# A fused decoder: the second half of a pair's scores ahead of the previous pair's weighed values

## The chip, the cores and the metric

The kernel runs on one core of one Trainium2 chip. The metric is the time of one execution in microseconds (us) on the device. The engines are TensorE (PE; PEld is its weight load), VectorE (DVE), ScalarE (ACT), GpSimd (POOL) and SyncE (SP, which issues the transfers).

## The reference, cut to what matters

Six stages follow each other, each with a residual and a layer norm: windowed self-attention (16 heads of 8), cross-attention to a context, a quantized product, a recurrence of 256 steps, a linear attention and an fp8 product. The change lies in the cross-attention of 8 batches (256 queries, 512 keys, 16 heads of 64):

```python
q = (lat @ Wq).reshape(b, n, HEADS, DHEAD).transpose(0, 2, 1, 3)
k = apply_rope(k, cos[None, None], sin[None, None])
attn = jnp.einsum('bhnd,bhsd->bhns', q, k) * scale
attn = jnp.clip(attn, -11.0, 11.0)
attn = jax.nn.softmax(attn, axis=-1)
out = jnp.einsum('bhns,bhsd->bhnd', attn, v)
```

## The kernel before, in words

Each engine has its own program, written by hand, and runs it strictly in the order written; semaphores tie the engines together. No scheduler or planner moves anything. Up to about 57 us the first batch is prepared, from 57 to 806 us the cross-attention runs, and then the later stages, which the change doesn't touch.

The cross-attention is a loop over 8 batches (0 to 7) and in each over 8 pairs of heads (0 to 7, `PAIRS`). A pair has two halves of 256 keys each. For a half, TensorE computes the scores of both heads (`unit(u)`, L2133, eight matmuls) into the same two banks, ScalarE takes the exponential (`exps(u)`, L1007) and VectorE clamps it (`clamp(u)`, L1471; the clip of the scores done behind the exponential). So `unit(1)` can only start when `exps(0)` has emptied the banks. GpSimd adds the four key blocks of the clamped tile in three additions (L731, L733, L735) to `psum`; TensorE multiplies values with the clamped tile (`values_of`, L2057) and sums `psum` over partitions (`sum_of`, L2065). VectorE divides (`attended`: reciprocal L1373, product L1374). These three work on the pair before, within the program of the current one.

Beside that, every pair prepares what later pairs need: keys of two pairs later in two products, "keys a" and "keys b" (L1758 to L1760, multiplied by cosine and sine on VectorE, L1315 and L1317, and added by GpSimd in `rotate`, L641, to `kr`), the queries of the next pair (from `lat_s`, the latents of the batch split into a high and a low part) and values. The `k_cos` and `k_sin` tiles are single, so the next `k_cos` waits for `rotate` (`kr_ready`).

In batches 0 to 6 the self-attention of the next batch is worked in between, cut into 48 slots, six for each pair: `slots(lo, hi)` stands in the pair's program on every engine and runs slots 6p+lo to 6p+hi-1 of that engine. Slots that matter here: 6, 8 and 10 (scores of the self-attention; VectorE reads them in L1251 and L1253 and frees the bank), 7 (`S_CN`: the normed context is turned and its high part kept, and VectorE makes its low part, L1305), 37 (`S_X1`: VectorE normalizes and measures x1, L1190, L1176 and L1179; GpSimd makes its reciprocal deviation, L624 and L626, and adds a bias, L692), 38 (latents normed on VectorE; GpSimd multiplies or adds a row to `k1`, L678), 40 (`S_RELU`, L1264), 43 (`S_LAT`: the latents are turned, and VectorE makes their low part, L1297, `lat_split`) and 44 (`S_KV_SUM`). The queries of the next batch's pair 0 are prepared near the end of pair 7, and wait for `lat_split`. The last batch has no slots.

Of the kernel before, what the change touches and what calls it, by code (L numbers as in the profile page):

```python
# [57 lines left out]
PER_PAIR = 6  # L58
SLOTS = PER_PAIR * PAIRS
S_X, S_K, S_Q, S_CTX, S_V = range(5)  # L60
S_CN = 7
S_MASKED = (3, 4, 5, 6)
S_SCORE = (6, 8, 10, 12, 14, 16, 18, 20)
S_EXP = (range(10, 14), range(14, 19), range(19, 24), range(24, 29))
# [115 lines left out]
def decoder(nc, a, out):  # L180
    with ExitStack() as ctx:
# [412 lines left out]
        def _(pool):  # L594
# [122 lines left out]
            def batch(b, last=False):  # L717

                for p in range(PAIRS):
                    pair = n(b, PAIRS, p)  # L720

                    def slots(lo, hi):
                        for i in range(lo, hi if not last else lo):
                            self_attention(b + 1, PER_PAIR * p + i, SELF_NORMS * (b + 1))

                    slots(0, 2)
                    pool.wait_ge(clamped, 2 * pair + 1)
                    if pair >= 2:
                        pool.wait_ge(o_full, pair - 1)
                    pp = prob[:, p % 2]  # L730
                    link(g.tensor_tensor(psum[:, p % 2, :], pp[:, 0, :], pp[:, 1, :], ALU.add))  # L731
                    pool.wait_ge(clamped, 2 * pair + 2)
                    link(g.tensor_tensor(psum[:, p % 2, :], psum[:, p % 2, :], pp[:, 2, :], ALU.add))  # L733
                    slots(2, 4)
                    g.tensor_tensor(psum[:, p % 2, :], psum[:, p % 2, :], pp[:, 3, :],  # L735
                                    ALU.add).then_inc(psum_ready, 1)
                    slots(4, 5)
                    if p + 2 < PAIRS or not last:
                        rotate(pair + 2)
                    if p == 0 and b >= 1:  # L740
                        rstd_of(b - 1, 0, QT, EPS_LN, ready=y_var_ready, done=y_rstd_ready)
                    slots(5, 6)
                    if last and p < B - 1:
                        rstd_of_f(p)
# [81 lines left out]
        def _(act):  # L826
# [170 lines left out]
            def batch(b, last=False):  # L997

                for p in range(PAIRS):
                    pair = n(b, PAIRS, p)  # L1000

                    def exps(u):
                        act.wait_ge(unit_full, 2 * pair + u + 1)

                        if pair >= 2 and u == 0:
                            act.wait_ge(o_full, pair - 1)
                        s.activation(prob[:, p % 2, 2 * u:2 * u + 2, :].rearrange("p k (h q) -> p h k q", h=2),  # L1007
                                     sc[:, 0:2, :].rearrange("p h (k q) -> p h k q", k=2), ACT.Exp,
                                     scale=DH ** -0.5).then_inc(exp_done, 1)

                    def slots(lo, hi):
                        for i in range(lo, hi if not last else lo):
                            self_attention(b + 1, PER_PAIR * p + i, SELF_NORMS * (b + 1))

                    def values_job(half):
                        if (b, p, f"values {half}") in JOB:
                            values(JOB[b, p, f"values {half}"], half)

                    exps(0)
                    slots(0, 1)  # L1020
                    slots(1, 2)
                    exps(1)
                    if p == PAIRS - 1:
                        values_job(0)
                        slots(2, 4)
                        values_job(1)
                        slots(4, 6)
                    if (b, p, "queries") in JOB:
                        queries(JOB[b, p, "queries"])
                    if p < PAIRS - 1:  # L1030
                        slots(2, 4)
                        values_job(0)
                        slots(4, 5)
                        values_job(1)
                        slots(5, 6)
                    if last and p == 1:
                        keep_turned(1, tail[:, 0:3, :].rearrange("p k d -> p (k d)"), bank_a[:, 0:3 * D])
                    if last and p >= 2:
                        keep_f(p - 2)
# [87 lines left out]
        def _(dve):  # L1127
# [97 lines left out]
            def self_attention(b, slot, norms):  # L1225
# [69 lines left out]
                if slot == S_LAT:  # L1295
                    dve.wait_ge(a_free, n(b, ACT_JOBS, SETUP_A + A_LAT + 1) if b >= 1 else FIRST_LAT)
                    w.tensor_tensor(lat_s[:, b % 2, 1, :], lat_raw[:, :], lat_s[:, b % 2, 0, :].bitcast(F32),  # L1297
                                    ALU.subtract).then_inc(lat_split, 1)
                if slot == S_CN:
                    if b == 0:  # L1300
                        dve.wait_ge(cn_kept, 1)
                    else:
# [41 lines left out]
            odd_turn(3)  # L1344
            measure_kv(0, 1)
            odd_turn(5)
            self_attention(0, S_CN, 0)
            odd_turn(7)
            odd_turn(9)
            invert_sums(0)  # L1350
# [111 lines left out]
            def batch(b, last=False):  # L1462

                for p in range(PAIRS):
# [17 lines left out]
                    keys_job("a")  # L1482
                    clamp(0)
                    slots(0, 1)
                    slots(1, 2)
                    if pair >= 1:
                        attended(pair - 1)
                    clamp(1)
                    slots(2, 3)
                    keys_job("b")  # L1490
                    slots(3, 4)
# [257 lines left out]
        def _(pe):  # L1749
# [367 lines left out]
            def batch(b, last=False):  # L2117

                for p in range(PAIRS):
# [37 lines left out]
                    unit(0)  # L2157
                    prep("keys a", prep_keys, "a")
                    slots(0, 1)
                    if pair >= 1:  # L2160
                        values_of(pair - 1)
                        sum_of(pair - 1)
                    slots(1, 2)
                    unit(1)
                    if p < PAIRS - 1:
                        prep("queries", prep_queries)
                        slots(2, 3)
# [287 lines left out]
```

## Time and profile before

| | |
|---|---|
| runs | 1050.55, 1050.72, 1046.6 us (median 1050.55) |
| profiled execution | 1047.62 us, its span 1045.9 us, mean granted clock 0.944 |
| TensorE | 919.8 us busy, 88% of the span |
| VectorE | 681.3 us, 65% |
| ScalarE | 509.6 us, 49% |
| GpSimd | 510.7 us, 49% |
| TensorE from 185 to 295 us | 103.77 of 110 us busy |

Busy shares say which engine has most work, not which wait ends last at a place; for that the timelines and waits are read. A matmul's row overlaps the next one's, since matmuls are pipelined, so work on TensorE is best measured from start to start. The granted clock is 1.00 at 2.4 GHz and 0.50 at 1.2 GHz.

### The profile page before, as it was taken

What the parts mean: (1) busy time and instruction counts of PE and PEld (TensorE: products, weight loads), DVE (VectorE), ACT (ScalarE), POOL (GpSimd) and SP (SyncE); (2) the same over time, 40 slices, a digit from 0 to 9 for tenths busy, and PEclk for the clock granted to TensorE, in tenths of its full rate; (3) what the DMA queues carried; (4) which work ended last, traced back from release to release, by engine and by line L of the source; (5) the groups of instructions that cost most, each with busy time, mean ns of one, the idle gap of its engine ahead of it and who ended that gap; (6) DMA issues with size and microseconds to landing.
All of it is one profiled execution on the core that took longest, in us unless ns stands there. A gap on an engine that the chain in (4) does not pass through costs nothing.

```text
span 1045.9 us, 22097 instructions
## 1 busy us (share of the span) xinstructions
PE 919.8 (88%) x8504; PEld 652.6 (62%) x8504; DVE 681.3 (65%) x1906; ACT 509.6 (49%) x1441; POOL 510.7 (49%) x642
## 2 busy tenths in 40 slices
PE   6689989998999999899989999998988499999922
PEld 4456656666665756566666666666656379888721
DVE  6446577568757766776687577667689543444477
ACT  6655645653663556456636645564233023333324
POOL 2643475356546534654565466446657112333363
PEclk9989999999999989999999999999999589999955
DMA  7000000000000000000000000000000001222211
GB/s 194 21 6 12 1 2 6 12 1 7 11 1 1 7 11 2 1 6 11 2 6 7 6 1 1 1 1 1 21 1 1 0 7 30 32 33 30 33 13 41
DMA packets 60470, 15.09 MB, mean 14 GB/s; under 512 B 41278, under 2 KB 59726, under 8 KB 60238
## 3 DMA queue, kind: packets, MB, share of 16 engines
q1 hardware_dynamic: 60366, 13.69, 6.1%
q8 instruction: 68, 1.11, 0.4%
q14 instruction: 36, 0.29, 0.1%
HBM read 10.51 MB, written 3.17 MB: 13 GB/s over the span
## 4 chain that ended last, share of the span: by engine, by line
PE 64%; DVE 19%; ACT 7%; POOL 5%; issue 3%; DMA 1%; SPq 0%; POOLq 0%; DVEq 0%; ACTq 0%
PE score_banks L2133 10%; PE out_bank L2057 8%; PE score_banks L1758 5%; DVE o_rec L1373 5%; PE bank_a L1753 5%; PE score_banks L2071 4%; DVE prob L1471 3%; PE score_banks L1789 3%; PE score_banks L1760 3%; PE score_banks L1759 3%; PE score_banks L2261 3%; PE bank_d L1774 3%; PE out_bank L2040 2%; PE out_bank L2065 2%; PE bank_d L2274 2%
## 5 line engine op out<-in xcount | busy, mean ns | idle before, releaser
L1007 ACT ACTIVATE prob<-score_banks 128x1024 f32<-128x1024 f32 x128 | 131.0, 1024 | 165.8 <-PE score_banks L2133 165.5
L733 POOL TENSOR_TENSOR psum<-psum,prob 128x512 f32<-128x512 f32 x64 | 81.6, 1275 | 153.9 <-DVE prob L1471 153.9
L2133 PE MATMUL score_banks<-qh,kr 64*128 64x256 f32 x1024 | 150.9, 415 | 2.1 <-ACT qh L916 1.3
L731 POOL TENSOR_TENSOR psum<-prob 128x512 f32<-128x512 f32 x64 | 82.6, 1290 | 98.4 <-DVE prob L1471 98.3
L1373 DVE RECIPROCAL o_rec<-out_bank 128x256 f32<-128x256 f32 x64 | 111.9, 1748 | 26.1 <-PE out_bank L2065 26.0
L2057 PE MATMUL out_bank<-prob,v 128*64 128x256 f32 x1024 | 124.7, 386 | 1.4 <-DVE on L1374 1.4
L2133 PEld LDWEIGHTS score_banks<-qh,kr 64*128 64x128 f32 x1024 | 91.9, 193 | 40.7 <-issue 30.5
L867 ACT ACTIVATE prob<-prob,neg_max 128x128 f32<-128x128 f32 (+1 forms) x256 | 107.1, 426 | 13.5 <-DVE neg_max L1258 13.5
L1471 DVE TENSOR_SCALAR prob<-prob 128x1024 f32<-128x1024 f32 x128 | 101.4, 792 | 12.9 <-ACT prob L1007 12.9
L2057 PEld LDWEIGHTS out_bank<-prob,v 128*64 128x64 f32 x1024 | 67.9, 136 | 46.6 <-issue 17.2
L1056 ACT ACTIVATE prob<-score_banks 128x8 f32<-128x8 f32 x255 | 45.1, 177 | 96.1 <-PE score_banks L2261 96.1
L1315 DVE TENSOR_TENSOR k_cos<-score_banks,cos_t 128x512 f32<-128x512 f32 x56 | 38.2, 682 | 72.4 <-PE score_banks L1760 46.2
L641 POOL TENSOR_TENSOR kr<-k_cos,k_sin 128x512 f32<-128x512 f32 x64 | 82.8, 1294 | 4.4 <-DVE k_sin L1317 3.6
L735 POOL TENSOR_TENSOR psum<-psum,prob 128x512 f32<-128x512 f32 x64 | 81.6, 1275 | 3.9
L2261 PE MATMUL score_banks<-prob,pt 128*64 128x8 f32 x1020 | 74.3, 210 | 0.6 <-ACT prob L1053 0.3
L835 ACT ACTIVATE pt<-bank_a 128x512 f32<-128x512 f32 x84 | 50.2, 598 | 35.5 <-PE bank_a L1753 34.6
L1774 PE MATMUL bank_d<-km,q 64*128 64x128 f32 x480 | 50.6, 330 | 17.9 <-DVE row_max L1253 16.6
L2261 PEld LDWEIGHTS score_banks<-prob,pt 128*64 128x64 f32 x1020 | 53.4, 137 | 20.8 <-ACT prob L1056 14.5
L2071 PE MATMUL score_banks<-w_qkv_t,ident 128*64 128x96 f32 (+1 forms) x336 | 64.8, 277 | 0.0
L1753 PE MATMUL bank_a<-ident,prob 128*128 128x128 f32 x360 | 57.0, 281 | 4.0 <-ACT pt L835 2.3
L1789 PE MATMUL score_banks<-pt,vm 128*32 128x128 f32 x768 | 54.0, 281 | 4.5 <-ACT pt L938 3.8
L760 POOL TENSOR_TENSOR var_eps<-mv,epsilons 128x1 f32<-128x1 f32 x49 | 9.5, 194 | 96.1 <-DVE mv L1575 96.1
(414 smaller groups left out, 2129.8 us busy)
## 6 DMA issues: line engine op xcount, KB each, us to landing
cb<-in_ctx_dram SPq DMA_DIRECT2D x8, 256.0 KB, 2.8
bias_mask<-bias_scratch SPq DMA_DIRECT2D x4, 384.0 KB, 5.4
xb<-in_x_dram SPq DMA_DIRECT2D x8, 128.0 KB, 2.1
prob<-in_L_xattn_Wkv_dram SPq DMA_DIRECT2D x1, 1024.0 KB, 8.4
x_scratch<-v SPq DMA_DIRECT2D x16, 64.0 KB, 1.5
bias_mask<-x_scratch SPq DMA_DIRECT2D x16, 64.0 KB
att_scratch<-on SPq DMA_DIRECT2D x16, 64.0 KB, 1.5
prob<-att_scratch SPq DMA_DIRECT2D x16, 64.0 KB, 3.0
```

The costliest lines, as they stand in the source:

```text
L641: g.tensor_tensor(kr[:, key % 2, :], k_cos[:, :], k_sin[:, :], ALU.add).then_inc(kr_ready, 1)
L731: link(g.tensor_tensor(psum[:, p % 2, :], pp[:, 0, :], pp[:, 1, :], ALU.add))
L867: last = s.activation(pr, pr, ACT.Exp, bias=neg_max[:, qt, j, g:g + 1], accum_out=row_sum[:, qt, j, g:g + 1])
L1007: s.activation(prob[:, p % 2, 2 * u:2 * u + 2, :].rearrange("p k (h q) -> p h k q", h=2), sc[:, 0:2, :].rearrange("p h (k q) -> p h k q", ...
L1373: link(w.reciprocal(o_rec[:, :], bank[:, T:2 * T]))
L1471: w.tensor_scalar(pr, pr, float(np.exp(-CLIP)), float(np.exp(CLIP)), ALU.max, ALU.min).then_inc(clamped, 1)
L1753: return nc.tensor.transpose(out_ap, in_ap, ident[0:in_ap.shape[0], 0:in_ap.shape[0]])
L1789: last = mm(o0_bank[32 * g:32 * g + 32, qt * P:(qt + 1) * P], vm[:, kt, j, 32 * g:32 * g + 32], pt[:, t % 2, i * P:(i + 1) * P], start=(j ...
L2057: mm(o[DH * h:DH * (h + 1), 0:T], v[:, (q // 2) % 2, kb, lo:lo + DH], prob[:, q % 2, kb, T * h:T * (h + 1)], start=(kb == 0), stop=(kb == ...
L2071: mm(bank[0:HALF_ROWS, 0:columns], ident[:, 0:HALF_ROWS], w_qkv_t[:, 0:columns], start=True, stop=True, skip_group_check=True)
L2133: last = mm(sc[:, h, k * T:(k + 1) * T], kr[rows_of, p % 2, kb * P:(kb + 1) * P], qh[rows_of, p % 2, :], start=True, stop=True, skip_group ...
L2261: last = mm(cf[lo:lo + HALF_ROWS, t * B:(t + 1) * B], a_t[:, lo:lo + HALF_ROWS], hid[:, (t - 1) * B:t * B], start=False, stop=True, skip_g ...
```

## The change

In a pair's program the second half's steps move ahead of the work on the pair before: on TensorE `unit(1)` ahead of `values_of`, `sum_of` and the pair's slot 1; on ScalarE `exps(1)` ahead of slot 1; on VectorE `clamp(1)` ahead of slot 1 and of `attended`, and `attended` ahead of slot 1. GpSimd's third addition moves ahead of the pair's slots 2 and 3. The low part of the normed context (slot 7 before) is made at slot 11 on VectorE alone. No instruction is added, removed or resized. The file is one line shorter, so behind L735 the same statement is numbered one less.

```diff
--- before.py
+++ after.py
@@ -58,7 +58,7 @@
 PER_PAIR = 6
 SLOTS = PER_PAIR * PAIRS
 S_X, S_K, S_Q, S_CTX, S_V = range(5)
-S_CN = 7
+S_CN, S_CN_LOW = 7, 11
 S_MASKED = (3, 4, 5, 6)
 S_SCORE = (6, 8, 10, 12, 14, 16, 18, 20)
 S_EXP = (range(10, 14), range(14, 19), range(19, 24), range(24, 29))
@@ -731,10 +731,9 @@
                     link(g.tensor_tensor(psum[:, p % 2, :], pp[:, 0, :], pp[:, 1, :], ALU.add))
                     pool.wait_ge(clamped, 2 * pair + 2)
                     link(g.tensor_tensor(psum[:, p % 2, :], psum[:, p % 2, :], pp[:, 2, :], ALU.add))
-                    slots(2, 4)
                     g.tensor_tensor(psum[:, p % 2, :], psum[:, p % 2, :], pp[:, 3, :],
                                     ALU.add).then_inc(psum_ready, 1)
-                    slots(4, 5)
+                    slots(2, 5)
                     if p + 2 < PAIRS or not last:
                         rotate(pair + 2)
                     if p == 0 and b >= 1:
@@ -1018,8 +1017,8 @@
 
                     exps(0)
                     slots(0, 1)
+                    exps(1)
                     slots(1, 2)
-                    exps(1)
                     if p == PAIRS - 1:
                         values_job(0)
                         slots(2, 4)
@@ -1296,7 +1295,7 @@
                     dve.wait_ge(a_free, n(b, ACT_JOBS, SETUP_A + A_LAT + 1) if b >= 1 else FIRST_LAT)
                     w.tensor_tensor(lat_s[:, b % 2, 1, :], lat_raw[:, :], lat_s[:, b % 2, 0, :].bitcast(F32),
                                     ALU.subtract).then_inc(lat_split, 1)
-                if slot == S_CN:
+                if slot == S_CN_LOW:
                     if b == 0:
                         dve.wait_ge(cn_kept, 1)
                     else:
@@ -1344,7 +1343,7 @@
             odd_turn(3)
             measure_kv(0, 1)
             odd_turn(5)
-            self_attention(0, S_CN, 0)
+            self_attention(0, S_CN_LOW, 0)
             odd_turn(7)
             odd_turn(9)
             invert_sums(0)
@@ -1482,10 +1481,10 @@
                     keys_job("a")
                     clamp(0)
                     slots(0, 1)
-                    slots(1, 2)
+                    clamp(1)
                     if pair >= 1:
                         attended(pair - 1)
-                    clamp(1)
+                    slots(1, 2)
                     slots(2, 3)
                     keys_job("b")
                     slots(3, 4)
@@ -2157,11 +2156,11 @@
                     unit(0)
                     prep("keys a", prep_keys, "a")
                     slots(0, 1)
+                    unit(1)
                     if pair >= 1:
                         values_of(pair - 1)
                         sum_of(pair - 1)
                     slots(1, 2)
-                    unit(1)
                     if p < PAIRS - 1:
                         prep("queries", prep_queries)
                         slots(2, 3)
```

VectorE in pair 6 of batch 1, before; `prob` in L1471 is the clamp, `o_rec` and `on` the division, `x` the normalization of slot 37 and `lat` that of slot 38:

```order
L1471 TENSOR_SCALAR prob<-prob 128x1024 [waits exp_done]
L1190 TENSOR_SCALAR x<-y,mv,rstd 128x128 [waits rstd_ready]
L1190 TENSOR_SCALAR x<-y,mv,rstd 128x128
L1176 BN_STATS stats<-x 128x6 [waits x1_ready]
L1176 BN_STATS stats<-x 128x6
L1179 BN_AGGR mv<-stats 128x2 [waits dve_chain]
L1179 BN_AGGR mv<-stats 128x2
L1373 RECIPROCAL o_rec<-out_bank 128x256 [waits on_ready,o_full]
L1374 TENSOR_TENSOR on<-out_bank,o_rec 128x256 [waits dve_chain]
L1471 TENSOR_SCALAR prob<-prob 128x1024 [waits exp_done]
```

After:

```order
L1470 TENSOR_SCALAR prob<-prob 128x1024 [waits exp_done] x2
L1372 RECIPROCAL o_rec<-out_bank 128x256 [waits on_ready,o_full]
L1373 TENSOR_TENSOR on<-out_bank,o_rec 128x256 [waits dve_chain]
L1189 TENSOR_SCALAR x<-y,mv,rstd 128x128 [waits rstd_ready]
L1189 TENSOR_SCALAR x<-y,mv,rstd 128x128
L1175 BN_STATS stats<-x 128x6 [waits x1_ready]
L1175 BN_STATS stats<-x 128x6
L1178 BN_AGGR mv<-stats 128x2 [waits dve_chain]
L1178 BN_AGGR mv<-stats 128x2
```

The second clamp joined the first, and the normalization and measurement of slot 37 moved behind the division.

VectorE in pair 7 of the same batch, before; `lat_s` is the low part of the latents (slot 43):

```order
L1315 TENSOR_TENSOR k_cos<-score_banks,cos_t 128x512 [waits kr_ready,p_full]
L1471 TENSOR_SCALAR prob<-prob 128x1024 [waits exp_done]
L1297 TENSOR_TENSOR lat_s<-x_t,lat_s 128x256 [waits a_free]
L1373 RECIPROCAL o_rec<-out_bank 128x256 [waits on_ready,o_full]
L1374 TENSOR_TENSOR on<-out_bank,o_rec 128x256 [waits dve_chain]
L1471 TENSOR_SCALAR prob<-prob 128x1024 [waits exp_done]
```

After:

```order
L1314 TENSOR_TENSOR k_cos<-score_banks,cos_t 128x512 [waits kr_ready,p_full]
L1470 TENSOR_SCALAR prob<-prob 128x1024 [waits exp_done] x2
L1372 RECIPROCAL o_rec<-out_bank 128x256 [waits on_ready,o_full]
L1373 TENSOR_TENSOR on<-out_bank,o_rec 128x256 [waits dve_chain]
L1296 TENSOR_TENSOR lat_s<-x_t,lat_s 128x256 [waits a_free]
```

The low part of the latents moved from ahead of the division to behind the second clamp and the division.

TensorE at the start of pair 7, before; `cn_s,wk_s` is keys a, `prob,v` the weighed values and `psum,ones` their sum of pair 6, `ident,lat` slot 43, and `qh,kr` (its last two rows) the second half's scores:

```order
L1758 MATMUL score_banks<-cn_s,wk_s 128x512 [waits p_free_by_act,cn_split]
L1759 MATMUL score_banks<-cn_s,wk_s 128x512
L1760 MATMUL score_banks<-cn_s,wk_s 128x512
L2057 MATMUL out_bank<-prob,v 64x256 [waits clamped,on_ready]
L2057 MATMUL out_bank<-prob,v 64x256 x3
L2057 MATMUL out_bank<-prob,v 64x256 [waits clamped]
L2057 MATMUL out_bank<-prob,v 64x256 x3
L2065 MATMUL out_bank<-psum,ones 64x256 [waits psum_ready]
L2065 MATMUL out_bank<-psum,ones 64x256
L1753 MATMUL bank_a<-ident,lat 128x128 [waits lat_ready,a_free]
L1753 MATMUL bank_a<-ident,lat 128x128
L2133 MATMUL score_banks<-qh,kr 128x256 [waits exp_done]
```

After:

```order
L1757 MATMUL score_banks<-cn_s,wk_s 128x512 [waits p_free_by_act,cn_split]
L1758 MATMUL score_banks<-cn_s,wk_s 128x512
L1759 MATMUL score_banks<-cn_s,wk_s 128x512
L2132 MATMUL score_banks<-qh,kr 128x256 [waits exp_done]
L2132 MATMUL score_banks<-qh,kr 128x256 x3
L2056 MATMUL out_bank<-prob,v 64x256 [waits clamped,on_ready]
L2056 MATMUL out_bank<-prob,v 64x256 x3
L2056 MATMUL out_bank<-prob,v 64x256 [waits clamped]
L2056 MATMUL out_bank<-prob,v 64x256 x3
L2064 MATMUL out_bank<-psum,ones 64x256 [waits psum_ready]
```

The second half's scores moved ahead of the values and their sum, and the wait for `exp_done` with them.

## Rows read from the trace of the kernel before

**Rows 1.** Windows of two batches: busy us of each engine, then granted clock (PEclk)
```profile
243.80:338.99 95.19, 89.28 (x690) 60.67 (x691) 66.36 (x174) 53.54 (x136) 51.65 (x54) 1.00 0.02 5
338.99:436.95 97.96, 92.20 (x690) 62.57 (x690) 66.40 (x174) 53.64 (x136) 51.65 (x54) 0.96 0.02 5
```

**Rows 2.** Waits of TensorE from 75 to 860 us: total us, times, longest
```profile
PE out_bank L2065 <- POOL psum L735: 16.7, 7, 2.4
PE bank_d L1774 <- DVE row_max L1253: 14.8, 7, 2.4
```

**Rows 3.** Timeline of TensorE: start, us, what, [idle before it <- releaser]
```profile
230.66 1.13 PE L2133 MATMUL score_banks<-qh,kr 64*128 64x256 f32 x8
...
232.61 1.95 PE L2057 MATMUL out_bank<-prob,v 128*64 128x256 f32 x16
234.39 0.60 PE L2065 MATMUL out_bank<-psum,ones 128*64 128x256 f32 x4
...
248.23 0.29 PE L1758 MATMUL score_banks<-lat_s,wq_s 128*128 128x256 f32 x1
...
249.08 0.50 PE L1758 MATMUL score_banks<-cn_s,wkx_s 128*128 128x512 f32 x1 [0.33 <-ACT v L910]
...
249.98 1.13 PE L2133 MATMUL score_banks<-qh,kr 64*128 64x256 f32 x8
```

**Rows 4.** Timeline of ScalarE: two exponentials of a pair's first half
```profile
231.84 1.03 ACT L1007 ACTIVATE prob<-score_banks 128x1024 f32<-128x1024 f32 x1 [0.92 <-PE score_banks L2133]
...
264.53 1.00 ACT L1007 ACTIVATE prob<-score_banks 128x1024 f32<-128x1024 f32 x1
```

**Rows 5.** Timeline of TensorE in pair 1 of batch 2
```profile
261.85 1.14 PE L2133 MATMUL score_banks<-qh,kr 64*128 64x256 f32 x8
...
264.56 1.95 PE L2057 MATMUL out_bank<-prob,v 128*64 128x256 f32 x16
...
273.59 0.82 PE L1774 MATMUL bank_d<-km,q 64*128 64x128 f32 x8 [2.08 <-DVE row_max L1253]
```

**Rows 6.** Timeline of GpSimd, pairs 6 and 7 of batch 1
```profile
236.31 0.20 POOL L624 TENSOR_TENSOR var_eps<-mv,epsilons 128x2 f32<-128x2 f32 x1 [2.01 <-DVE mv L1179]
...
237.94 1.28 POOL L731 TENSOR_TENSOR psum<-prob 128x512 f32<-128x512 f32 x1
239.91 1.28 POOL L733 TENSOR_TENSOR psum<-psum,prob 128x512 f32<-128x512 f32 x1 [0.69 <-DVE prob L1471]
...
243.71 1.45 POOL L641 TENSOR_TENSOR kr<-k_cos,k_sin 128x512 f32<-128x512 f32 x1
```

**Rows 7.** Timeline of VectorE, pairs 6 and 7 of batch 1, pair 1 of batch 2
```profile
233.33 1.52 DVE L1471 TENSOR_SCALAR prob<-prob 128x1024 f32<-128x1024 f32 x1
234.78 0.59 DVE L1190 TENSOR_SCALAR x<-y,mv,rstd 128x128 f32<-128x128 f32 x2
...
236.08 1.73 DVE L1373 RECIPROCAL o_rec<-out_bank 128x256 f32<-128x256 f32 x1
237.84 0.42 DVE L1374 TENSOR_TENSOR on<-out_bank,o_rec 128x256 f32<-128x256 f32 x1
...
242.56 1.47 DVE L1264 TENSOR_SCALAR k<-k 128x512 f32<-128x512 f32 x1 [0.69 <-POOL k L678]
245.26 0.69 DVE L1315 TENSOR_TENSOR k_cos<-score_banks,cos_t 128x512 f32<-128x512 f32 x1 [1.23 <-POOL kr L641]
245.87 0.68 DVE L1471 TENSOR_SCALAR prob<-prob 128x1024 f32<-128x1024 f32 x1
246.47 0.42 DVE L1297 TENSOR_TENSOR lat_s<-x_t,lat_s 128x256 fp32r<-128x256 f32 x1
...
269.65 1.75 DVE L1373 RECIPROCAL o_rec<-out_bank 128x256 f32<-128x256 f32 x1
```

**Rows 8.** Timeline of TensorE in the last pair of the last batch
```profile
797.46 1.13 PE L2133 MATMUL score_banks<-qh,kr 64*128 64x256 f32 x8
...
803.77 1.95 PE L2057 MATMUL out_bank<-prob,v 128*64 128x256 f32 x16 [1.43 <-DVE on L1374]
```

## The prediction

> **What bounds the kernel now.** I read the page first, then TensorE's waits, then the timelines of all engines around the longest ones. In the cross-attention TensorE is the bound: a batch without disturbance lasts 95.19 us from one wait to the same wait of the next batch, and TensorE is busy for 89.28 of them [rows 1]. Two waits per batch make up most of the rest. In pair 7 `sum_of` waits for GpSimd's third addition, 16.7 us in seven times, so 2.39 each; in pair 1 the third score product of the self-attention waits for VectorE to free its bank, 14.8 us in seven times, so 2.11 [rows 2]. So the most that better order can bring is about 4.5 us per batch, and whatever the change makes late on the way to TensorE costs in full, since TensorE has almost no slack elsewhere. The timelines count more than the busy shares here: VectorE and GpSimd are idle for a third to a half, but each waits in program order.
>
> **The scores.** ScalarE starts on a first half 1.18 us behind the start of its product and needs 1.03 (231.84 against 230.66), so the banks are free 2.21 us behind it. A blocked product starts some 0.05 us later, an estimate for the hand-over [rows 3, 4]. Today the next work starts after 1.95 us (232.61). In a pair without work in its slot 0 `unit(1)` therefore waits 0.3 us; where slot 0 has a product, nothing. Pairs 6 and 7 pay it in places where something later decides anyway (below); pair 4 pays it openly, and its next slot has a turn whose copy by ScalarE now comes directly ahead of the next turn. I take 0.5 us per batch for pairs 0, 2, 3, 4 and 5 together, an estimate; 0 if ScalarE's own queue absorbs it, 1.5 if each of the five pays one such stall. No weight load or matmul is added.
>
> **Pair 1, the gain.** TensorE reaches its values 2.71 us behind this pair's start (264.56 against 261.85). ScalarE, held by the context's norm, is through with the pair's first exponential only at 265.53 [rows 4, 5]. So `unit(1)` waits for 0.97, or 0.9 if the norm comes a little earlier, and so does all behind it. On VectorE the division then begins at 261.85 + 3.63 + 1.06 + 1.78 + 0.65 = 268.97, where it begins at 269.65 now [rows 7]. From there to the release of the bank are 3.94 us now (to 273.59, [rows 5]), 0.61 of them a clamp that will stand ahead: released at 272.3. TensorE comes there at 273.59 - 2.08 + 0.9 = 272.4: the wait is gone, and 1.2 us are gained per batch. That VectorE has room for this ahead of the division: the low part of the context is gone (0.6), and GpSimd's chain of the y norm comes one addition earlier (1.28, [rows 6]).
>
> **Pairs 6 and 7, the loss.** Here two steps of the self-attention, slot 37 and slot 43, now stand behind the division on VectorE, and the division stands behind TensorE's `unit(1)`. I follow it in batch 1, whose pair 6 starts at 230.66.
> Step 1. `unit(1)` starts at 230.66 + 2.26 = 232.92 and lasts 1.06 (1.13 less the overlap), the values 1.78 (232.61 to 234.39), the sum reaches VectorE another 0.65 later: 236.41 [rows 3]. The second clamp fits before it. The reciprocal takes 1.76 and the product 0.34 until the next start, so 238.51. There the x normalization begins, which now begins at 234.78 [rows 7]. Step 1 is 3.73 us late.
> Step 2. GpSimd's slot 37 waits for that measurement already now (2.01 us, [rows 6]), and the three additions, the affine row, and `rotate` are queued behind it. Its start goes from 236.31 to 240.04. The second addition doesn't wait for its clamp any more (0.69 now) and saves 0.62 of that, with 0.07 left for the hand-over. `rotate` so starts at 243.71 + 3.73 - 0.62 = 246.82 instead of 243.71, ends 248.27, and `k_cos` of pair 7 starts at 248.35 instead of 245.26 [rows 6, 7]. `psum` of pair 6 is complete at 241.67 + 1.35 x 3 = 245.7, against 243.7 now (the start of `rotate` behind it): the very addition that was put first comes later. The step at slot 40 waits too (0.69 now), to about 246.9, and holds the keys' sum of slot 44 on TensorE until some 248.4.
> Step 3. From `k_cos` to the latents' low part are 1.21 us now (245.26 to 246.47). Behind the change a second clamp (0.61) and the division (2.13) lie between: it starts at 248.35 + 1.21 + 2.74 = 252.30 and ends at 252.65.
> Step 4. TensorE starts the next batch's queries when that is split: 252.75 instead of 248.23, 4.52 us later. Until the next pair's start it needs 1.75 now, 0.33 of them a wait for ScalarE [rows 3] that is gone by then, and 0.1 for a first matmul behind an idle time; so pair 0 of the next batch starts at 254.06 instead of 249.98. **The loss is 4.1 us per batch**, and the old wait of 2.39 is within it, moved and not removed.
>
> Everything from step 1 to 4 is one chain, so each microsecond by which the measurement of slot 37 is less late comes back in full, down to the slack of the latents of 1.3 us (246.89 to 248.23).
>
> One clamp takes 0.68 us alone and 1.52 where GpSimd is within an instruction (233.33, 245.87) [rows 7]. The Trainium skill says in SBUF — State Buffer, "SBUF: two separate sides", that the pair of ports that VectorE and GpSimd share is an exclusive lock, held for a whole instruction by whoever starts first. Adjacent clamps and adjacent additions meet more often by that rule; the trace agrees with it at 233.33. By the rows a meeting costs up to 0.84 us; I count it once, in the slot 40 step, where it lies beside `rotate`. If each of steps 1 and 3 met one more, the chain would be 1.7 longer per batch.
>
> **The last batch** has no slots. In its pairs 0 to 5 the new order changes little: the second clamp and the division both stand ahead of `k_sin`, in either order. In pairs 6 and 7 there are no keys a, so `unit(1)` waits 1.2 us (2.26 - 1.06), and pair 7 starts 1.1 later, at 798.6. Its division starts 2.26 + 1.06 + 1.78 + 0.65 = 5.75 behind that, and is through at 806.45; the last values wait for it and now start at 803.77 [rows 8]. That is 2.7 us, less some 0.2 gained ahead: 2.5, with bounds 0 and 4.
>
> **The sum.** Seven batches with slots: 7 x (4.1 + 0.5 - 1.2) = 23.8. Last batch 2.5. The profiled execution took 1047.6 us (span 1045.9), 2.9 below the median of the three runs (1050.55). 1047.6 + 26.3 = 1073.9; with 1 us for the clock, below, **1075 us**. What measurement can tell from no change is about 0.5%, 5 us.
>
> **Rivals.**
> *The clock.* TensorE idles 2.75 us ahead of the queries and 2.9 ahead of the sum, closer together than today's waits. A batch with a half-speed spell behind such a wait lasts 97.96 at a mean granted clock of 0.96, against 95.19 at 1.00 [rows 1], so up to 2.8 each. If all seven batches had a spell of that size in the open, that is 19 us, less 8 if three of the seven have one today (an estimate; one of the two batches in the rows has it): 1085. The Trainium skill's rule in TensorE: Matmul & The Clock Gate, "HAM oscillation", is that idle gaps let the clock fall again and again, which would do just this; no row shows waits in this new pattern.
> *Only one delay bites.* If VectorE reaches the second clamp and the division of pair 7 before `k_cos` is due to hold it, step 3 adds nothing (2.74 less): 1075 - 7 x 2.7 = 1056. Against it: `k_cos` is ahead of both in program order and waits for GpSimd already now (1.23, [rows 7]).
> *Faster.* The wait for the sum goes and the latents are in time: 7 x (2.39 + 1.2 - 0.5) = 21.6 gained, 2.5 lost at the end: 1028. It is decided at one place, the latents' low part: it would have to be less than about 2 us later than now, its slack of 1.3 and what pair 1 gives back net. I find 5.8. For it: VectorE is idle for a third of the time, and might come through the division before I think, if the values' sum is there sooner.
> *Nothing changes.* Losses and gains of 1 to 2 us per batch cancel: 1048 to 1052.
>
> **How the numbers follow.** Forecast 0.66 (its own range 1066 to 1082), the clock 0.14, only one delay 0.08, faster 0.09, no change 0.03. The range reaches over the first three cases and leaves out 0.12 and some of the edges: 1055 to 1086. Slower by over 0.5% are forecast, clock and nearly all of the one delay: 0.86; within 0.5% 0.05; faster 0.09.
>
> **What the profile would show.** Right: in pair 7 TensorE's queries (L1757) wait some 2.7 us for VectorE's `lat_s` (L1296), seven times, a group of waits that doesn't exist now; `sum_of` still waits 2 to 3 us for GpSimd; L1773 behind `row_max` is nearly gone; `unit(1)` has waits of 0.3 for the exponential and one of 0.9 in pair 1; a batch lasts about 98.6. Wrong: no wait for `lat_s`, or GpSimd's L624 of slot 37 at the same place in the batch as now. Then step 1 is the one that failed.

## The result, and the profile after

The changed kernel takes 1072.21 us (median of five runs, 1070.1 to 1082.97) against 1048.51 us for the kernel before (five runs on the same chip, 1046.6 to 1050.72): the ratio is 1.0245, 95% interval 1.0192 to 1.0298. It is slower by 24 us, where 1075 was forecast. The profiled execution is the slowest of the five (1082.97 us, mean granted clock 0.926; the others had 0.936 to 0.941), so single rows are read in an undisturbed batch of it and totals from the medians.

The page of the changed kernel (busy us, share of the span):

```profile
span 1081.3 us, 22090 instructions
...
PE 934.5 (86%) x8504; PEld 665.9 (62%) x8504; DVE 671.5 (62%) x1906; ACT 518.1 (48%) x1441; POOL 516.5 (48%) x642
```

Every engine runs as many instructions as before (8504, 1906, 1441 and 642). The waits of TensorE, 75 to 900 us (total, times, longest), answer to [rows 2]:

```profile
PE out_bank L2064 <- POOL psum L734: 20.3, 7, 2.9
PE score_banks L2132 <- ACT prob L1006: 17.3, 35, 3.8
PE score_banks L1757 <- DVE lat_s L1296: 13.9, 7, 2.5
PE score_banks L1757 <- DVE k_sin L1316: 6.5, 10, 1.1
PE bank_a L1752 <- ACT pt L834: 4.7, 14, 0.3
...
PE bank_d L1773 <- DVE row_max L1252: 2.2, 7, 0.3
```

The wait for the sum did not go, it grew from 2.4 to 2.9 us. The wait for the row maximum is nearly gone. The group `lat_s`, seven times and up to 2.5 us, did not exist before. The group `prob` is `unit(1)` waiting for the exponential of the first half; its 3.8 us are one place at the loop's start, the others are 0.2 to 1.1.

Windows from one wait for the sum to the next (columns as in [rows 1]):

```profile
354.73:453.23 98.50, 90.07 (x690) 61.70 (x691) 65.60 (x173) 54.70 (x136) 52.52 (x54) 0.98 0.02 5
651.72:750.25 98.53, 90.07 (x690) 61.69 (x691) 65.60 (x173) 54.72 (x136) 52.51 (x54) 0.98 0.00 1
152.94:254.30 101.36, 93.12 (x691) 63.55 (x691) 65.34 (x173) 54.73 (x136) 52.45 (x54) 0.95 0.02 5
```

Against the clean batch of [rows 1] a batch is 3.3 us longer: TensorE is busy for 0.8 us more and idle for 2.5 us more. TensorE's timeline in pairs 6 and 7, then pairs 0 and 1 of the next batch, with one product from pair 1 of the batch before, answers to [rows 3, 5]:

```profile
287.04 0.82 PE L1773 MATMUL bank_d<-km,q 64*128 64x128 f32 x8
...
341.93 1.14 PE L2132 MATMUL score_banks<-qh,kr 64*128 64x256 f32 x8 [0.23 <-ACT prob L1006]
...
354.73 1.12 PE L2064 MATMUL out_bank<-psum,ones 128*64 128x256 f32 x4 [2.90 <-POOL psum L734]
...
362.01 0.39 PE L1757 MATMUL score_banks<-lat_s,wq_s 128*128 128x256 f32 x1 [2.45 <-DVE lat_s L1296]
...
363.26 1.13 PE L2132 MATMUL score_banks<-qh,kr 64*128 64x256 f32 x8
...
375.05 1.14 PE L2132 MATMUL score_banks<-qh,kr 64*128 64x256 f32 x8
...
378.73 1.13 PE L2132 MATMUL score_banks<-qh,kr 64*128 64x256 f32 x8 [0.90 <-ACT prob L1006]
```

The chain between them, first on VectorE, then on GpSimd; it answers to [rows 6, 7]:

```profile
347.56 0.59 DVE L1189 TENSOR_SCALAR x<-y,mv,rstd 128x128 f32<-128x128 f32 x2
...
355.93 1.48 DVE L1263 TENSOR_SCALAR k<-k 128x512 f32<-128x512 f32 x1 [3.25 <-POOL k L678]
357.33 0.68 DVE L1314 TENSOR_TENSOR k_cos<-score_banks,cos_t 128x512 f32<-128x512 f32 x1
357.93 1.28 DVE L1470 TENSOR_SCALAR prob<-prob 128x1024 f32<-128x1024 f32 x2
359.13 1.75 DVE L1372 RECIPROCAL o_rec<-out_bank 128x256 f32<-128x256 f32 x1
...
361.25 0.70 DVE L1296 TENSOR_TENSOR lat_s<-x_t,lat_s 128x256 fp32r<-128x256 f32 x1
```

```profile
349.10 0.20 POOL L624 TENSOR_TENSOR var_eps<-mv,epsilons 128x2 f32<-128x2 f32 x1 [5.79 <-DVE mv L1178]
...
353.42 1.26 POOL L734 TENSOR_TENSOR psum<-psum,prob 128x512 f32<-128x512 f32 x1
...
355.86 1.27 POOL L641 TENSOR_TENSOR kr<-k_cos,k_sin 128x512 f32<-128x512 f32 x1
```

GpSimd's wait for the measurement of slot 37 went from 2.01 to 5.79 us; the three additions, `rotate`, `k_cos`, two clamps, the division and only then the latents' low part stand in a line behind it.

### The profile page after: what moved, and what is told of

The parts are those of the page before. It is cut to its first block, busy times and chain, and to the rows that moved or that the text cites. A ratio compares the mean times of both kernels' runs of the same rounds, so it can differ in the third digit from the quotient of the medians.

```text
span 1081.3 us, 22090 instructions
## 1 busy us (share of the span) xinstructions
PE 934.5 (86%) x8504; PEld 665.9 (62%) x8504; DVE 671.5 (62%) x1906; ACT 518.1 (48%) x1441; POOL 516.5 (48%) x642
## 4 chain that ended last, share of the span: by engine, by line
PE 62%; DVE 19%; POOL 7%; ACT 7%; issue 4%; DMA 0%; SPq 0%; POOLq 0%; DVEq 0%; ACTq 0%
PE score_banks L2132 11%; PE out_bank L2056 10%; DVE o_rec L1372 6%; PE bank_a L1752 4%; PE score_banks L1757 4%; PE score_banks L2070 4%; PE score_banks L1788 4%; PE score_banks L2260 3%; ACT prob L1006 3%; PE bank_d L1773 3%; PE score_banks L1758 2%; PE score_banks L1759 2%; PE out_bank L2064 2%; PE bank_d L2273 2%; DVE stats L1175 2%
## 5 line engine op out<-in xcount | busy, mean ns | idle before, releaser
L731 POOL TENSOR_TENSOR psum<-prob 128x512 f32<-128x512 f32 x64 | 85.0, 1328 | 109.0 <-DVE prob L1470 108.8
L2056 PE MATMUL out_bank<-prob,v 128*64 128x256 f32 x1024 | 128.0, 393 | 1.9 <-DVE on L1373 1.9
L1470 DVE TENSOR_SCALAR prob<-prob 128x1024 f32<-128x1024 f32 x128 | 96.9, 763 | 36.4 <-ACT prob L1006 36.4
L624 POOL TENSOR_TENSOR var_eps<-mv,epsilons 128x2 f32<-128x2 f32 (+2 forms) x37 | 7.2, 196 | 111.7 <-DVE mv L1178 111.6
L2064 PE MATMUL out_bank<-psum,ones 128*64 128x256 f32 x256 | 41.4, 404 | 20.3 <-POOL psum L734 20.3
```

The costliest lines, as they stand in the source:

```text
L1470: w.tensor_scalar(pr, pr, float(np.exp(-CLIP)), float(np.exp(CLIP)), ALU.max, ALU.min).then_inc(clamped, 1)
L2056: mm(o[DH * h:DH * (h + 1), 0:T], v[:, (q // 2) % 2, kb, lo:lo + DH], prob[:, q % 2, kb, T * h:T * (h + 1)], start=(kb == 0), stop=(kb == ...
```

## The experiments

The ratio is to the kernel before, timed beside each. "Batch" is the distance between starts of the same output product of TensorE, most common value in the profile.

| kernel | us | ratio, 95% | batch |
|---|---|---|---|
| before | 1048.5 | | 95.2 to 99.5 |
| changed | 1072.2 | 1.0192 to 1.0298 | 98.5 to 101.4 |
| 1 slot 37 ahead of the division | 1058.6 | 1.0078 to 1.0127 | 97.2 |
| 2 slot 43 ahead of the division | 1058.1 | 1.0075 to 1.0129 | 97.2 |
| 3 both | 1038.0 | 0.9879 to 0.9921 | 94.4 |
| 4 scores and low part alone | 1058.9 | 1.0076 to 1.0128 | 96.4 to 98.0 |
| 5 slot 1 behind the division alone | 1063.1 | 1.0089 to 1.0170 | 98.9 |
| 6 additions alone | 1041.6 | 0.9900 to 0.9942 | 95.5 |
| 7 low part alone | 1041.6 | 0.9891 to 0.9952 | 95.6 |
| 8 as 3, last batch old | 1034.5 | 0.9822 to 0.9896 | 94.4 |
| 9 changed, fillers | 1067.3 | 1.0124 to 1.0228 | 98.55 |
| 10 as 8, fillers | 1036.1 | 0.9834 to 0.9931 | 94.47 |
| 11 additions and low part | 1024.5 | 0.9728 to 0.9811 | 93.0 |
| 12 low part, fillers | 1031.3 | 0.9772 to 0.9872 | 94.1 |

### Which step behind the division costs: 1 to 3

All start from the changed kernel. Experiment 1 on VectorE (2 is the same with `p == 7`, 3 without the condition):

```diff
                     clamp(1)
+                    if p == 6:
+                        slots(1, 2)
                     if pair >= 1:
                         attended(pair - 1)
-                    slots(1, 2)
+                    if not (p == 6):
+                        slots(1, 2)
```

> The changed kernel, with one thing undone: in pair 6 of every batch VectorE runs slot 37 (and only that) ahead of the division again, behind the second clamp. Chain theory: the measurement of x1 comes 2.7 us earlier in each of seven batches (from behind the division to behind the clamp), so GpSimd's additions, the next k_cos and the latents' low part come 2.7 earlier and the wait of TensorE for the sum falls from 2.9 to about 0.3; a batch lasts about 95.8 instead of 98.5, the kernel 1053. Rival (the 35 waits of unit(1) for the exponential, 17.3 us, are what costs, and the place of the self-attention's slots is not): 1070 to 1074, no change.

> The changed kernel, with the other thing undone: in pair 7 of every batch VectorE runs slot 43 (the latents' low part) ahead of the division, behind the second clamp. Chain theory: the low part comes 2.1 us earlier, so the wait of TensorE's queries falls from 2.45 to about 0.3, while the wait for the sum stays at 2.9; a batch lasts about 96.4, the kernel 1057. Rival (the exponential's waits): 1070 to 1074.

> The changed kernel with VectorE's slot 1 ahead of the division in all pairs, so both steps at once. Chain theory: 2.7 + 2.1 = 4.8 us of the chain are gone, down to TensorE's own work and the slack; wait for the sum about 0.3, wait for the latents 0.9; a batch lasts about 93.2, less than the 95.2 of the kernel before, and the kernel 1035 to 1038 (last batch 2.5 us longer than before). Rival (the exponential's waits): 1070 to 1074. Rival (both delays cover one another, only one counts): 1053.

Measured: 1058.6, 1058.1 and 1038.0 us. TensorE's waits, experiment 1, then experiment 2, then 3:

```profile
PE score_banks L1760 <- DVE lat_s L1296: 18.3, 7, 2.6
...
PE bank_d L1890 <- DVE k L1263: 7.8, 7, 1.1
```

```profile
PE out_bank L2067 <- POOL psum L734: 20.4, 7, 2.9
...
PE score_banks L1760 <- DVE lat_s L1296: 6.1, 6, 1.3
```

```profile
PE score_banks L2132 <- ACT prob L1006: 13.8, 35, 1.1
PE score_banks L1757 <- DVE lat_s L1296: 8.9, 7, 1.3
PE bank_d L1887 <- DVE k L1263: 7.7, 7, 1.1
```

Slot 37 ahead takes the wait for the sum away and leaves that for the latents; slot 43 ahead leaves the sum and cuts the latents' wait to less than half. Each gives 14 us. Both give 34, more than the two together: in experiment 3 the granted clock is 1.00 in every batch but the first, and the half-speed rows, priced at 5 us by experiment 9, are gone too.

The batches of experiments 1 and 2 lasted 97.2 to 97.3 us, where 95.8 and 96.4 were expected; those of experiment 3 lasted 94.43, where 93.2 was expected. In experiment 1 the clock was 0.98 in every batch, with rows of half speed behind the wait for the latents (a score product of 1.75 us at 348.80). Its miss of 5 us in the whole time is of that size, and experiments 9 and 12 come back to it. The clock does not explain the other two: experiment 2 has batches of 97.20 us at 1.00 and at 0.98 alike. There the trace shows another cause, which the expectations had left out. The latents' low part now stands directly behind the clamps, and the first of them lets GpSimd begin an addition. In experiment 3:

```profile
338.01 1.65 POOL L731 TENSOR_TENSOR psum<-prob 128x512 f32<-128x512 f32 x1 [1.56 <-DVE prob L1470]
...
338.46 1.48 DVE L1296 TENSOR_TENSOR lat_s<-x_t,lat_s 128x256 fp32r<-128x256 f32 x1
```

The subtraction lasts 1.48 us beside that addition, in experiment 2 too, against 0.42 in [rows 7] and 0.70 in the changed kernel. This 1.06 us is about what each of the two batches is too long by (0.8 and 1.2). That the meeting is the cause is read from the rows and was not tested by a run of its own.

With both steps undone the change is faster than the kernel before: the whole loss is in these two steps.

### The parts alone: 4 to 7

Each is the kernel before with one part of the diff of the section on the change: 4 the moves on TensorE and ScalarE and the low part at slot 11; 5 VectorE's slot 1 behind `attended` and `clamp(1)`, which keep their old order; 6 GpSimd's hunk; 7 the hunks with `S_CN_LOW`.

> The kernel before with the move on TensorE and ScalarE and the context's low part at slot 11, but with VectorE's old order (slot 1, division, second clamp) and GpSimd's old order. Chain theory: slots 37 and 43 are in time, so no wait for the latents; the wait for the sum stays near 2.4 less 1; unit(1) waits for the exponential as in the changed kernel (17 us in all); per batch 0.9 gained in pair 7, 0.8 in pair 1, 0.5 lost elsewhere, 2.5 lost in the last batch: about 1043. Rival (the exponential's waits are what costs): 1065 to 1072.

> The kernel before, with one thing of the change alone: on VectorE the division and the second clamp stand ahead of slot 1, nothing moves on TensorE, ScalarE or GpSimd. Chain theory: in pair 6 the measurement of x1 comes 3.0 us later and in pair 7 the latents' low part stands behind division and clamp; TensorE's wait for the sum goes from 2.4 to 4.8 and the queries start 3.9 us later; a batch lasts about 98.4, the kernel 1071. Rival (the order on VectorE costs only because TensorE's unit(1) comes first): 1048 to 1053.

> The kernel before, with GpSimd's three additions adjacent and nothing else. Chain theory: the affine row no longer lies between the second and third addition, so the wait for the sum falls from 2.4 to 1.2 and nothing else takes its place (the latents are split 0.1 us ahead of the queries): a batch lasts 94.0, the kernel 1040. Rival (the gain is taken back by the wait for the latents or for the keys' sum): 1048.

> The kernel before, with the low part of the normed context at slot 11 of VectorE and nothing else. Theory: VectorE saves 0.95 us ahead of the third score product of pair 1 (0.6 of work and a wait of 0.36 for ScalarE), so TensorE's wait for the row maximum falls from 2.1 to 1.1: a batch lasts 94.2, the kernel 1042. Rival (the division's wait for the sum fills the place): 1048.

Experiment 4 was a miss: 1058.9 us. Its longest groups of waits:

```profile
PE score_banks L2133 <- ACT prob L1007: 17.6, 34, 1.6
PE score_banks L1758 <- DVE k_sin L1317: 15.1, 14, 1.9
PE bank_d L1774 <- DVE row_max L1253: 10.6, 14, 0.9
PE out_bank L2065 <- POOL psum L735: 6.9, 7, 1.0
```

There is no wait for the latents at all, so the slots were in time. But where the second clamp stays behind the division and the sum comes later on TensorE, that clamp, `k_sin` and the reads of the self-attention's scores are late instead: the wait for `k_sin` rose from 4.2 (experiments 5 to 7) to 15.1. I had counted the second clamp as free in either order. In the seven batches with slots these waits only eat the gain that was expected: together they last 676.3 us, 675.2 before. The loss against the kernel before is nearly all in the last batch: from its start to its last values 79.63 us, against 70.68 before and 74.32 in experiment 3.

So the scores' move seems to need the clamp's move, but this isn't separated. Experiment 3 (1038.0) differs from experiment 4 in the adjacent additions too. As the wait for the sum is 6.9 us in all here, they can take away no more than that of the 21 us between the two by this wait.

Experiment 5 went the way forecast, by 15 of the 22 us: 1063.1. The wait for the sum is at its longest here, and GpSimd waits for the same measurement as in the changed kernel:

```profile
PE out_bank L2065 <- POOL psum L735: 33.3, 7, 4.8
...
338.23 0.20 POOL L624 TENSOR_TENSOR var_eps<-mv,epsilons 128x2 f32<-128x2 f32 x1 [5.02 <-DVE mv L1179]
```

So the second clamp and the division ahead of slot 1 do the harm without any move of scores. Its batches are 98.9 us against 95.2 in the clean one before, 3.7 each; but the mean batch before is 96.3 (481.56 us for five, 161.68 to 643.24), and 2.6 x 7 = 18 is nearer to what was measured. Its expectation was 8 us too long; that it left out the slow batches which the kernel before has anyway is my reading, and covers about that much.

Experiments 6 and 7 gave what was expected, 1041.6 each.

### Last batch, clock, and the two small edits together: 8 to 12

Experiment 8 is experiment 3 with, on TensorE (and the same on VectorE for the second clamp):

```diff
-                    unit(1)
+                    if not last:
+                        unit(1)
                     if pair >= 1:
@@
                     slots(1, 2)
+                    if last:
+                        unit(1)
```

> The version with slot 1 ahead of the division on VectorE (1038), and in the last batch alone the order of before on TensorE and VectorE. Theory: the second half of pairs 6 and 7 of the last batch no longer waits for the exponential with nothing between, 2.5 us less: 1035.5. Rival (those waits are hidden, the end of the last batch is bound by other work): 1038.

1034.5 against 1038.0: the last batch costs 3.5 us of the change. The intervals of the two ratios overlap, so the size is not firm; the traces give 2.2 from the start of the last batch to its last values (74.32 and 72.13).

Experiments 9, 10 and 12 put small matmuls of the kernel's own filler kind, which write a spare bank, in front of a waiting instruction. One such filler is two matmul instructions in the trace. Experiment 12, in full (9 and 10 likewise, at the places that the texts name):

```diff
                         values_of(pair - 1)
+                        for _ in range(6 if p == PAIRS - 1 and not last else 0):
+                            keep_clock()
                         sum_of(pair - 1)
```

> The changed kernel with TensorE's idle times in pair 7 filled with 16 of the kernel's own small filler matmuls per batch: 8 ahead of the sum of squares, 2 behind the values of head 0, 6 ahead of the next queries; the last batch has none. The waits for GpSimd and VectorE stay, so what is left to gain is the half-speed matmuls behind them: the changed kernel's batches were 98.5 us where the granted clock was 0.97 to 0.98, and 100.0 to 101.4 us where it was 0.95 to 0.96. If the idle time of 2.9 and 2.5 us brings those half-speed stretches, all batches come to 98.5 us: 1061 to 1066 us. If they do not hang on it, 1072 us, and over 1075 if the fillers themselves push the chain.

> Slots 37 and 43 behind the second clamp but ahead of the division in all pairs, the old order in the last batch, and 6 filler matmuls per batch around pair 7 on TensorE. Its batches were 94.44 us without fillers, and 91.31 us once. If the 3.1 us between the two is half-speed matmuls that idle time brings, six or seven batches come to 91.3 to 92.5 us: 1018 to 1030 us. If the clock does not answer to these fillers, 1034.5 us.

> The kernel before with two of the small edits and none of the others: the two additions of GpSimd adjacent, and the low part of the context at the later slot. Alone they gave 1041.6 us each, by different waits: the additions cut the wait for the sum from 2.4 to 1.2 us per batch (16.7 to 8.2 us in seven), the low part that for the row maximum (14.8 to 7.4 us in seven). If the two add up, 1034 to 1035 us. The rival is that one wait takes the place of the other, because both hang on one chain of VectorE: 1038 to 1041 us.

> The low part of the context at the later slot alone (1041.6 us; batches of 95.6 us at a granted clock of 0.98), and 6 filler matmuls ahead of the sum in pair 7, where TensorE waits 2.4 us and half-speed rows stand behind it. If the two small edits gave more together than apart because a half-speed spell had taken back the gain of each alone, the spell of 1.5 us goes in each batch: batches of 94.0 us at 1.00, 1030 to 1032 us. If it was something else, 1041 us, and batches of 95.6.

Experiment 9: 1067.3 us. Its waits and two of its batches:

```profile
PE score_banks L1757 <- DVE lat_s L1296: 3.6, 7, 0.5
...
PE out_bank L2064 <- POOL psum L734: 2.3, 7, 0.3
```

```profile
164.51:263.06 98.55, 94.33 (x725) 64.93 (x723) 65.66 (x174) 54.66 (x137) 52.57 (x54) 1.00 0.02 5
263.06:361.61 98.55, 94.32 (x725) 64.93 (x723) 65.61 (x174) 54.64 (x137) 52.55 (x54) 1.00 0.02 5
```

These rows say two things. TensorE is now never idle for long at those places and has the full clock in every batch, and yet a batch lasts 98.55 us, as the clean one without fillers did. So its length is set by the chain through VectorE and GpSimd, not by TensorE. And the batches of 100 to 101 us are gone: behind those waits stood half-speed matmuls, worth 5 us in all (1072.2 to 1067.3). The intervals of the two ratios overlap, though each of the five runs of the one is above all four of the other, so the 5 is weaker than the clock column.

With this clean batch the two delays can be priced without the clock: 98.53 us here, 97.20 with slot 43 ahead (experiment 2), 94.43 with slot 37 ahead too (experiment 3). So slot 43 costs 1.3 us per batch, net of the longer subtraction that its other place brings, and slot 37 another 2.8; seven times both is 29, and with the 5 us of the clock it is the 34 of experiment 3.

Experiment 10 changed nothing (1036.1), since experiment 8 already ran all batches with slots but the first at 1.00. Its expectation rested on one batch of 91.3 us that was no batch; from the second on, those with slots last 94.5.

Experiment 11 was a surprise: 1024.5 us, where the sum of two gains of 7 is 1034.5. Windows between the same output products of experiment 6, of 7, and of 11:

```profile
351.25:446.78 95.53, 90.98 (x692) 61.88 (x691) 66.25 (x174) 53.64 (x137) 51.56 (x53) 0.98 0.02 5
```

```profile
350.35:445.93 95.58, 90.72 (x692) 61.32 (x691) 68.41 (x174) 53.53 (x137) 51.64 (x54) 0.98 0.02 5
```

```profile
251.85:344.82 92.97, 89.50 (x691) 60.76 (x690) 67.00 (x174) 53.55 (x137) 51.49 (x53) 1.00 0.02 6
```

The clean batch before is 95.19 us. Each edit takes a wait of about 1.2 us away and should give 94.0; instead 6 and 7 have a clock of 0.98 and 95.5 to 95.6. In experiment 7 the place is seen behind the wait that remains:

```profile
525.70 1.12 PE L2065 MATMUL out_bank<-psum,ones 128*64 128x256 f32 x4 [2.40 <-POOL psum L735]
...
527.37 2.08 PE L2133 MATMUL score_banks<-qh,kr 64*128 64x256 f32 x8
```

Those rows last twice their usual 0.60 and 1.13. Experiment 12 fills this wait and nothing else (a row of the timeline, then the wait that is left):

```profile
234.57 2.11 PE L2071 MATMUL bank_d<-w_qkv_t,ident 128*64 128x192 f32 x12
```

```profile
PE out_bank L2065 <- POOL psum L735: 3.1, 7, 0.4
```

```profile
251.51:345.65 94.14, 91.23 (x704) 62.26 (x703) 67.15 (x174) 53.57 (x137) 51.72 (x54) 1.00 0.02 5
```

Batches of 94.14 at 1.00 and 1031.3 us, as expected: ten us less than experiment 7 (by the ratios, 0.9822 and 0.9921, whose intervals do not meet), 1.5 per batch, from six fillers that compute nothing. So the two edits give more together than apart because each alone leaves a wait of 2.1 to 2.4 us per batch with a half-speed stretch behind it, and both together leave only waits of 1.2 and no such stretch (1.00 in the windows of experiment 11). For the low part experiment 12 shows this. For the additions it is read from the rows alone: in experiment 6 pairs 1 and 2, where the wait for the row maximum is left, last 27.3 us together, against 26.0 in the clean batch before.

This is in line with the rule in TensorE: Matmul & The Clock Gate of the Trainium skill, "HAM oscillation", that idle time lets the clock fall again and again. The waits of the page's own case are longer than the 2.40 us that were enough here.

## Why the prediction was right, by its own steps

The loss sits where it was put, and the rows after can be laid beside the steps. Times from the start of pair 6 (339.67 after, 230.66 in the prediction's rows):

| step | predicted | after |
|---|---|---|
| 1 normalization of slot 37 starts | 7.85 | 7.89 |
| 2 GpSimd's L624 | 9.38 | 9.43 |
| 2 `psum` complete | 15.04 | 15.01 |
| 2 `rotate` starts | 16.16 | 16.19 |
| 2 `k_cos` of pair 7 | 17.69 | 17.66 |
| 3 latents' low part starts | 21.64 | 21.58 |
| 4 queries of the next batch | 22.09 | 22.34 |
| 4 pair 0 of the next batch | 23.40 | 23.59 |

Up to the start of the low part nothing is off by more than 0.06 us, and then 0.25: the low part takes 0.70 us here, against 0.42 in [rows 7]. The loss of pairs 6 and 7 is 23.59 - 19.32 = 4.3 us per batch (4.1 predicted). The queries wait 2.45 us for it (2.7 predicted).

*Pair 1.* `unit(1)` waits 0.90 (0.9). The third score product starts 10.49 us behind the pair (287.04 in that batch, whose pair 1 starts at 276.55), 11.74 before: 1.25 gained by then (1.2). The whole pair lasts 12.15 us, 13.60 before: 1.45 gained.

*Pairs 0 and 2 to 5.* From pair 0 to pair 6 a batch takes 438.17 - 363.26 = 74.91 us, before 75.87 (with the start of the next pair 6 put at 230.66 + 95.19). With pair 1's 1.45 this leaves a loss of 0.5, as was taken: pairs 2, 3 and 4 are 0.17, 0.19 and 0.23 longer, pair 0 is 0.09 shorter and pair 5 unchanged. The open stall is in pair 4, 0.23.

*The batch.* 98.50 to 98.53 us, 98.6 forecast; 3.3 longer than 95.19, 3.4 by the sum.

*The last batch.* Forecast 2.5; experiment 8 gives 3.5 by the medians and 2.2 by the rows. Its last values:

```profile
827.72 1.14 PE L2132 MATMUL score_banks<-qh,kr 64*128 64x256 f32 x8
...
835.74 3.62 PE L2056 MATMUL out_bank<-prob,v 128*64 128x256 f32 x16 [1.95 <-DVE on L1373]
```

They start 8.02 us behind the pair, 6.31 before [rows 8]; with pair 6 (7.82 long, 6.63 before) that is 2.9. Pair 5 is 0.6 longer (9.93, 9.33 before), where the prediction had little change in pairs 0 to 5, and pairs 3 and 4 together are 1.5 shorter. In this execution the product then ran at half speed, 3.62 against 1.95; in experiment 3 it did not.

*The clock.* This term was mis-sized, by some 4 us and in its sign. It stood in the sum as one more microsecond. The kernel before has 1.1 us per batch of half-speed time, 96.31 against 95.19, about 8 us in seven. The changed kernel has 5, by experiment 9. So 1048.5 + 7 x 3.3 + 3.5 - 3 = 1072, which is what it takes; as the last two terms are each known to a microsecond or so, no closer agreement can be claimed. That 1075 came within 3 us of it is partly luck: the clock was 4 too high and the seven batches 0.7, the last batch up to 1 too low and the start (1047.6) 0.9. The reason it fell short of the rival: the matmuls at half speed behind the wait for the sum stand ahead of the wait for the latents, and are paid by it. The windows of 98.50 us have a clock of 0.98 and last no longer than those at 1.00 in experiment 9. I had that cover in view nowhere.

*The ports.* The prediction counted one meeting of VectorE and GpSimd and allowed for more. On the chain of the changed kernel one more is seen, at the low part (0.70 us for 0.42); the large one, 1.48, came only where that step was moved (experiments 2, 3, 8 and 10).

*The rivals.* "Only one delay bites" is excluded by the `lat_s` row and by experiments 1 and 2, which price each delay at 14 us. "Faster" needed the low part under 2 us later; experiment 3 makes it so, and is faster. What the prediction didn't see is how good two small parts of the change are: the additions and the low part alone are worth 24 us, the moved scores and second clamp cost 10 of it even in the best order (experiment 8 against 11), the last batch 3.5, and the slots behind the division 34.

## What to carry to other kernels

When two blocks change places in a program that runs in order, follow the one that moved back to its last consumer on another engine, and ask which queue it feeds there: here a second clamp and a division ahead of a measurement made it 3.8 us late, and through GpSimd's queue the very sum that was to come earlier. Test parts in pairs as well as alone: two edits of 7 us gave 24, since the wait that is left can keep the clock low and take back part of what the other edit gained. Before a step is moved next to another, look what the other releases: the low part of the latents behind the clamp lasted 1.48 us instead of 0.42, beside the GpSimd addition that the clamp had let go. Where TensorE waits for something else anyway, a few matmuls into a spare bank show, and sometimes win, what the clock takes.

## What was not expected of the hardware

The same wait brings half-speed matmuls in one batch and none in the next. In the kernel before a wait of 2.07 us for the row maximum (at 368.77) is followed by rows of double length in the batch of 99.50 us (a `unit` of 2.08 at 371.72), and two batches later (at 563.46) a wait of 2.08 at the same place is followed by rows of the usual length (0.82 for the product, 1.14 for the `unit`). With one wait shortened (experiments 6 and 7) the half-speed stretch came in nearly every batch, and cost 1.5 us in each. So a shorter wait can have the lower clock; what decides it beside the waits was not separated here.
